# First scan of a two-layer state-space and expert kernel: the B product of each pair's second half kept in PSUM

## What is computed

```python
# state space: for each channel d and each of 16 states n
dA  = exp(delta * A)                 # A = -exp(A_log)
dBx = (delta * xn) * Bm              # Bm: one row of values over time for each n
def step(h, inp):
    dA_t, dBx_t, C_t = inp
    h = dA_t * h + dBx_t             # the scan
    return h, einsum('bdn,bn->bd', h, C_t)
# experts: every token goes to 4 of 16 experts
h = silu(x @ w_gate.T) * (x @ w_up.T)
acc = acc + h @ w_d.T * cw[:, None]
```

## Time and profile before

| | us |
|---|---|
| median of 3 runs | 1246.53 |
| lowest and highest of them | 1244.57, 1248.17 |
| the profiled execution, its own time | 1250.39 |
| its span, first to last instruction | 1248.6 |

### The profile page before, as it was taken

One profiled execution on the slowest core, in us unless ns is written; L12 is line 12 of the kernel. 1 busy time (PEld: TensorE's weight loads), 2 busy tenths in 40 slices (PEclk: granted clock), 3 DMA queues, 4 the chain that ended last, 5 costly groups with the idle time before them and its releaser, 6 DMA issues.

```text
span 1248.6 us, 18530 instructions
## 1 busy us (share of the span) xinstructions
PE 1013.1 (81%) x6024; PEld 590.7 (47%) x6024; DVE 915.4 (73%) x1506; ACT 490.4 (39%) x1114; POOL 450.2 (36%) x333
## 2 busy tenths in 40 slices
PE   3987997778888887765677768999989988889895
PEld 2354455444444444434334534555555554555453
DVE  4758667999998989996486655776667566755486
ACT  2200226455554454540221054534554344444442
POOL 0000102888887878750450102322222222223210
PEclk9989999999998889986888889999999999998898
DMA  6950352877878877977700233433333333234324
GB/s 223 368 143 1 102 106 86 158 149 150 166 150 150 158 145 146 163 132 206 168 5 0 44 84 85 109 79 92 92 84 84 85 80 88 69 84 108 80 31 136
DMA packets 107091, 143.25 MB, mean 115 GB/s; under 512 B 30022, under 2 KB 97334, under 8 KB 102710
## 3 DMA queue, kind: packets, MB, share of 16 engines
q0 software_dynamic: 30368, 77.92, 32.1%
q1 hardware_dynamic: 76630, 64.14, 18.5%
HBM read 72.80 MB, written 39.46 MB: 90 GB/s over the span
## 4 chain that ended last, share of the span: by engine, by line
PE 45%; DVE 24%; issue 9%; DMA 8%; POOL 7%; ACT 6%; ACTq 0%; SPq 0%; DVEq 0%; POOLq 0%
PE bank L686 6%; DMA sum<-yo,to_i 5%; PE bank L1844 4%; PE bank L1433 4%; PE bank L1426 4%; PE bank L698 4%; POOL sum L1163 3%; DVE xnT L1144 3%; PE bank L1888 3%; POOL xg L1170 3%; PE bank L1827 2%; PE bank L1874 2%; DVE cv L2089 2%; PE bank L1910 2%; PE bank L1836 2%
## 5 line engine op out<-in xcount | busy, mean ns | idle before, releaser
L1498 POOL DMA_INDIRECT sum<-yo,to_i x48 | 77.8, 1621 | 355.8 <-ACT yo L1453 351.0
L1170 POOL DMA_INDIRECT xg<-xn_d,token_i x80 | 103.8, 1297 | 176.8 <-DVE to_i L460 93.9
L1163 POOL DMA_INDIRECT sum<-yo,to_i x80 | 148.1, 1851 | 39.6 <-DMA sum<-yo,to_i 19.4
L1011 PE MATMUL bank<-areaA,xgT 128*128 x320 | 123.8, 513 | 15.1 <-issue 9.6
L1028 PE MATMUL bank<-areaA,hidT 88*128 x320 | 92.8, 414 | 40.5 <-ACT hidT L1076 34.4
L2034 DVE TENSOR_TENSOR areaD<-areaD,gb 128x512 f32<-128x512 f32 x128 | 87.4, 689 | 39.4 <-ACT areaD L1981 34.5
L1144 DVE TENSOR_TENSOR_SCAN xnT<-areaB,xnT 128x1024 f32<-128x1024 f32 x42 | 96.2, 2290 | 3.3
L1981 ACT ACTIVATE areaD<-bank 128x512 f32<-128x512 f32 x128 | 76.1, 594 | 44.1 <-PE bank L1836 42.5
L1028 PEld LDWEIGHTS bank<-areaA,hidT 88*128 88x128 f32 x320 | 56.0, 195 | 74.7 <-issue 70.1
L686 PE MATMUL bank<-xnT,areaB 128*128 128x512 f32 x192 | 86.8, 599 | 0.8 <-DVE y L716 0.8
L1011 PEld LDWEIGHTS bank<-areaA,xgT 128*128 128x128 f32 x320 | 58.3, 200 | 58.4 <-issue 42.2
(11 more groups left out here) (338 smaller groups left out, 2164.4 us busy)
## 6 DMA issues: line engine op xcount, KB each, us to landing
y<-xnT POOLq DMA_DIRECT2D x21, 1024.0 KB
wst<-gu_f SPq DMA_DIRECT2D x96, 176.0 KB
y<-areaB POOLq DMA_DIRECT2D x11, 1024.0 KB
wst<-down_f SPq DMA_DIRECT2D x48, 176.0 KB
areaA<-in_gu SPq DMA_DIRECT2D x2, 2816.0 KB
gu_f<-in_gu POOLq DMA_DIRECT2D x1, 5632.0 KB, 17.2
sum<-yo SPq DMA_DIRECT2D x2, 2176.0 KB, 16.4
down_f<-in_down POOLq DMA_DIRECT2D x1, 2816.0 KB, 23.0
```

The costliest lines, as they stand in the source:

```text
L1011: last = nc.tensor.matmul(bank[:, GB + q % 2, 0:2 * FI], xgT[:, q % 2, k, :], wgu0_of(e, k), start=(k == 0), stop=(k == KD - 1))
L1163: nc.gpsimd.indirect_dma_start(sum0_d[q % 2], bass.IndirectOffsetOnAxis(ap=to_i[:, q:q + 1], axis=0), yo[:, q % 5, :], None, compute_op=AL ...
L1170: nc.gpsimd.indirect_dma_start(xg[:, q % 5, :], None, xn_d[0], bass.IndirectOffsetOnAxis(ap=token_i[:, q:q + 1], axis=0)).then_inc(s.gathe ...
L1498: nc.gpsimd.indirect_dma_start(sum1_d, bass.IndirectOffsetOnAxis(ap=to_i[:, q:q + 1], axis=0), yo[:, q % 4, :], None, compute_op=ALU.add). ...
```

## The change

The B multiply of the units with `hf` 1 writes its result over row B in PSUM banks 0 and 1, and the scan of these units reads it there; the scan's output still goes to `h` in SBUF. Units with `hf` 0 are as before. So the next pair's B product, which overwrites these banks, waits for the scan of the pair's second unit (`da_free`) and no longer for its B multiply (`bx_done`), and stands one tick later in TensorE's queue, at the head of that tick.

```diff
         def b_product(pe, pair):
 
             if pair:
-                pe.wait_ge(bx_done, 2 * pair)
+                pe.wait_ge(da_free, 2 * pair)
             rows_product(pe, pair // 2, BROW, pair, b_full)
@@ layer0_tensor
             for t in range(TICKS0):
                 q, part = divmod(t, TILE)
+                pair = (t + 1) // (2 * UNIT)
+                if t % (2 * UNIT) == 2 * UNIT - 1 and pair < UN // 2:
+                    b_product(pe, pair)
                 if part == 1 and q < NT0:
                     hid_transposes(pe, q)
                 if part == 1 and q + 2 < NT0:
                     x_transposes(pe, q + 2)
-                pair = (t + 2) // (2 * UNIT)
-                if t % (2 * UNIT) == 2 * UNIT - 2 and pair < UN // 2:
-                    b_product(pe, pair)
                 if t and t % (2 * UNIT) == 0:
                     c_product(pe, t // (2 * UNIT))
@@ layer0_vector
                 h = h_pair[pair % 3][:, hf, :]
+                bx = both(BROW) if hf else h
@@
-                    nc.vector.tensor_tensor(h, dx[:, hf, at], both(BROW), ALU.mult).then_inc(bx_done, 1)
+                    nc.vector.tensor_tensor(bx, dx[:, hf, at], both(BROW), ALU.mult).then_inc(bx_done, 1)
@@
-                    nc.vector.tensor_tensor_scan(h, dA[:, u % 2, :], h, 0.0, ALU.mult, ALU.add).then_inc(da_free, 1)
+                    nc.vector.tensor_tensor_scan(h, dA[:, u % 2, :], bx, 0.0, ALU.mult, ALU.add).then_inc(da_free, 1)
```

## The result

The changed kernel takes 1236.22 us (median of 6 runs, 1233.16 to 1239.87) beside 1246.28 us for the kernel before in the same comparison (6 runs, 1243.44 to 1248.17). The ratio is 0.9922, with a 95% interval of 0.990 to 0.9944. The forecast was 1255.1 with a range from 1247, so sign and range are both wrong.

The account below looks back on a forecast made before the run. VectorE was taken to set the stage, losing time to silus waiting for a late tanh behind a TensorE chain. The terms 0 + 2.7 + 0 + 5.9 = 8.6 us on the median 1246.53 gave 1255.1, range 1247 to 1265.

Parts of the forecast that it names:

- VectorE's own instructions: 32 B multiplies writing to PSUM and 32 scans reading it keep their times: 0 us.
- Rival 3: VectorE writing over the bank it reads runs at half rate: 34 us more, 1289; chance 0.04.
- Term A: Ticks 22 and 23: B product waits for the scan, gate_up comes 0.3 us later in nine loops: 2.7 us lost.
- Term B: Ticks 14 and 15: B product between down and gate_up delays gate_up 0.60 us, which fits before the silu: 0.
- Term C: TensorE's clock: longer, single pauses at ticks 22 to 23 and 14 bring more half clock: 5.9 us lost.
- GpSimd: Scatter-adds held up less by scans, but nothing in the stage waits for GpSimd: 0.
- rival 2: GpSimd's relief reaches the path through a late gather and the last scatter-add: 4.5 us gained, 1242.0; chance 0.09.
- Rival 1: TensorE's clock stays as it is, only the order costs: 2.7 us lost, 1249.2; chance 0.20.
- Rival 4: VectorE's next B multiply would wait for the late B product; costs nothing measurable, 1246.5; chance 0.07.

Follow-up runs that it names:

- e1: Kernel before with only the B product's move and new wait (da_free), all operands in SBUF; ratios 0.9978, 0.9976 and 0.9963 in three runs.
- r2: Second run of e1 (move and new wait alone, all operands in SBUF), beside the changed kernel on the same chip; ratio 0.9976.
- e5: Changed kernel with gate_up issued ahead of the C product at ticks 24k; 1236.70 us, ratio 0.9896 to the kernel before.
- e7: e5 with all operands in SBUF (`bx = h`), so gate_up first without PSUM operands; ratio 0.997 to the kernel before.
- f2: e1 with six unread extra matmuls in each of two TensorE pauses, ahead of tick 23's B product and tick 14's down; ratios 0.9984 and 1.0006.
- f1: Kernel before with six unread extra matmuls in each of two TensorE pauses, ahead of tick 14's down and tick 24's C product; ratio 0.999.

## Where the prediction failed

**VectorE's own instructions, 0.** Right: 1222 and 2287 ns. Rival 3 (34 us) is out, and so is the estimate of 2.1 us for the scans by the Trainium skill, VectorE: DVE Perf Modes, section The TRN2 errata.

**Term A, 2.7 us: direction right, size not.** Down came 0.76 us after the B product as said, and the C product 0.96 after that. Then I let gate_up follow by 0.60 to 0.75 us, the distance behind a product that had waited. The C product no longer waited, and gate_up followed by 0.43. From the scan's end to gate_up it is 2.13 us before (307.86 to 309.99) and 2.20 after (306.69 to 308.89): 0.07 us a loop, 0.6 in all.

**Term B, 0: right.** gate_up came 0.58 us after the B product (296.36), and no silu of tick 17 waited except behind the one half-clock gate_up at 330.02, by 0.90 us. What I did not follow is where those 0.6 us go next.

**Term C, +5.9 us: the step that failed, in sign.** It had two errors. The first is in the numbers: I took the transposes ahead of tick 22 to end where they ended before, and so a pause of 1.9 us. They come later, because all that is behind tick 15's gate_up does. The pause is 1.04 us in the third loop and 0.98 to 1.34 in nearly all of the changed kernel's, in place of 0.51 and 1.19. I had moved the product in one place of the timeline and left the rest of it standing. The second is in the reasoning: that the seven falls behind the pauses of ticks 22 to 24 stay, and that longer pauses only add to them. Of the ten slow gate_ups before, nine are those of ticks 0 and 3; after, one is. The pause at tick 14 did grow, from 0.94 to 1.37 us, in every loop, and here the forecast had the direction: none of ten gate_ups behind it was slow before, 2 of 30 in the changed kernel's three profiles and 8 of 30 in e1's three. It was the size that was off, with one (330.02) where I took three. At tick 23, pauses of 1.12 and 1.13 us in r2 were followed by half clock, and in the 27 loops of the changed kernel's three profiles one was. The half-clock stretches went from 9 to 2; the waits for tanh shrank by 7.5 us in place of growing by 8.8, and these 7.5 are the stage's 7.3.

**GpSimd, 0, and rival 2: the second step that failed.** The holds did become shorter (1851 to 1781 ns), as the rule of the Trainium skill, SBUF - State Buffer, section Who interferes with whom, has it. I put their effect at nothing because no wait in the stage names GpSimd, and gave the rival 0.09. The PSUM operands brought 0.36 to 0.46%, 4.5 us by the medians of one chip, and the only path that the traces show for it starts at GpSimd: an addition issued late, a register load of 0.9 us in place of 0.3, a late down. No wait names it, since the table shows the last releaser of a wait and not what made that releaser late, and a slow register load stands there as "issue". Rival 2's time, 1242.0, was the nearest, and by luck: its terms were not the ones. The wait of 2.7 us at tick 5 of loop 7 is still 1.65 us (at 452.92), and the last scatter-add was not what counted.

**Rival 1** (the clock as it was) is out by the table at the top. **Rival 4** is out too: no B multiply waits for its product in either kernel.

## What to carry over

When an instruction is moved in a queue, write the timeline forward to the end of the loop, not only at the place: here 0.6 us of delay at tick 15 filled a pause at tick 22. Where a stage has a chain that is late in every loop, treat the clock as unknown in sign, with the gain of all its falls undone as one end of the range (here 7 us) and not only new falls. And give an operand that can stay in PSUM for nothing a real chance to help: the order with gate_up first was at 0.9896 with PSUM operands (e5) and at 0.997 with SBUF operands (e7). Where "issue" grows ahead of an instruction, look at the register load in its queue and at what the DMA engines move at that moment.

## What the runs showed of the hardware

- VectorE may read a bank and write over it at the rate of the form that writes to SBUF: 1222 ns beside 1214 for 128 x 1024.
- The same program can run a stage in two patterns: 361.6 and 372.2 us in two executions of f2, with a down product that starts 0.79 to 1.00 us after the product ahead of it in the one and 1.35 to 1.38 us in seven loops of the other. One profile doesn't tell which a median (0.9984, 1.0006) stands for.
- A register load on TensorE or ScalarE took 0.90 us on average while 8 KB packets filled the DMA engines, and 0.36 us with 1 KB packets (1906 and 1029 loads in 20 profiles).
- A pause of TensorE's doesn't tell by its length alone whether the clock falls: 1.37 us at tick 14 kept full clock in 28 of 30 loops of the changed kernel's profiles, while in r2 1.13 us were followed by 0.50. Filling pauses raised the mean granted clock (f1 0.9378 beside 0.9308) and bought 0.1% at most.
